# Mean and variance of the first layer norm on ACT for three of four chunks, with the order of all items changed

## The chip, the cores and the metric

One core of a Trainium2 chip runs the whole program. Time is device microseconds of one execution; what counts is the median over several runs. The engines are TensorE (PE), VectorE (DVE), ScalarE (ACT), GpSimd (POOL) and SyncE (SP, which here only issues DMAs). Each runs its own instruction list in order, and they meet through semaphores.

## What is computed

Four sequences (chunks) of 512 tokens, 128 features. Each goes through an attention-like block and a mixture of experts:

```python
mod = (_silu(c) @ wmod).reshape(4, 6, 1, -1)      # sa, ca, ga, sb, cb, gb per chunk
h = _layernorm(x) * (1 + ca) + sa
x = x + ga * attn(h)                              # rmsnorm, in-projection, two convolutions,
                                                  # gate, low-rank mixing, out-projection
h = _layernorm(x) * (1 + cb) + sb
logits = h @ router_w.T + expert_bias             # top 8 of 160, sigmoid weights, normalised
routed = sum over experts of combine * silu(h @ w_gate[e]) @ w_down[e]
x = x + gb * (routed + shared)
```

The first `_layernorm` is (x - mean) / sqrt(var + 1e-5) over the 128 features of each token.

## The kernel before, in words

A chunk is four tiles of 128 tokens (NT = 4), tokens on the partitions. The experts are taken in pairs, two pairs to a **duo**: 40 duos a chunk, 160 in all. For duo J the PE runs the up projection of two pairs (`up`, three fp16 matmuls of 128x512 each, since every fp32 operand is split into a high and a low half), ACT evicts each with silu (L859, into `s_all`), DVE multiplies by the combine weights (`gm`, L1169), ACT writes the high half (`gh`, L878, into `g_all`), DVE the low half (`gl`, L1158), and PE adds the down projection into one bank. The down projection of duo J - 4 is interleaved with the up projection of duo J (LAG = 4), gh and gl of duo J - 2 with silu and gm of duo J (HOLD = 2). There are two up banks, so an up projection waits for the silu of the duo before in its bank.

Everything else is a named **item**: `setup(n)` prepares weights, `att(c, name)` is a step of the block of chunk c or of the router, `split_hi(k)` on ACT and `split_lo(k)` on DVE turn weight piece k into its halves (20 pieces, L723 and L986). One function, `walk`, gives the order for all engines. It first lists items by hand (the start), then runs the duos, and after duo d of chunk c it takes the items in the table `WITH[c][d]`. Every engine walks this same list and emits only its own part of an item, so moving an item moves it on each engine that takes part in it. The order is fixed when the program is built.

Items that matter here, in the order of the data:

- `stat` (L987 to L1003 on DVE, L651 on POOL): for the first norm of chunk c, four BN_STATS, four BN_AGGR and `ve` = variance + 1e-5 on DVE, then POOL raises it to -0.5 (`rstd`). `nb` (L1012): -mean * rstd.
- `t1a`, `t1b` (ACT, L732), `hm`, `ha` (DVE, L1030, L1033): the normalised and modulated `h`. Chunk 0 does it on DVE alone (L1018, L1025). For chunks 1 to 3 `hm` needs the modulation rows, which `setup(20)` and `setup(22)` send through DRAM (SP: `rows_mod`, then the broadcast into `mod`, L535 and L538).
- `square` (ACT, L739, with an accumulator), `rms` (DVE L1008, POOL L654), `hi` (ACT, L744), `turn` (PE), `hnT` (ACT, L758), `low` (DVE, L1050): the rms norm and the transposed input in two halves.
- `conv`, `val`, `z`, `gate` (PE); `mid0/1` (ACT, L777) and `tap0/1:0` to `:8` (DVE, L1058 and L1065): the 9-tap convolution of each half of the features, on PE for one half of chunks 0 and 1 and on DVE for the others. `zh` (ACT), `zl` (DVE, L1082), `zmv` (SP, four DMAs, L566).
- `silu0/1` (L768, L765), `tanh0/1` (L784), `gy0/1` (DVE, L1088), `ya`, `yb`, `o0`, `o1` (PE), `x2` (DVE, L1093): the end of the block. `wo` and `base0/1` prepare it.
- `bn` (DVE, L1097), `rstd2` (POOL, L657), `nb2` (L1109), `t2a/t2b` (ACT, L793), `turn2` (PE, L1373), `xh` (ACT, L815 and L816), `xl` (DVE, L1117): the second norm, transposed, in two halves: the input of all 40 duos of the chunk.
- `logit` and `shup` (PE), `prob` (ACT, sigmoid, L822, with a table load), `max`, `sum`, `swap` (DVE), `norm` (ACT, L846), `cw` (DVE, L1142): the combine weights. For chunk 0 `c0` and `c1` (ACT L838, PE L1417) spread the weights of the first two duos. `ss`, `ssh` (ACT, L829, L832) and `ssl` (DVE) are the shared expert's input.

The start does the whole block of chunk 0 and much of that of chunk 1; the rest of chunk 1 and the blocks of chunks 2 and 3 are spread over the duos by the table.

Of the kernel before, what the change touches and what calls it, by code (L numbers as in the profile page):

```python
# [18 lines left out]
NT = L // P  # L19
# [47 lines left out]
for _n, _w in (("id", P), ("ones2", P), ("isym", L), ("esym", EDGE)):  # L67
# [11 lines left out]
        4: ((11, "split_lo"), (12, "split_hi"),),
        6: ((12, "split_lo"),),  # L80
        7: ((1, "silu1"),),
        8: ((2, "t1a"), (2, "hm"), (13, "split_lo"), (1, "yb0"), (1, "tanh0"), (3, "nb"), (1, "ya1"), (2, "t1b"),
            (13, "split_hi"),),
        10: ((2, "ha"),),
        11: ((14, "split_lo"), (14, "split_hi"), (15, "split_hi"), (15, "split_lo"), (1, "tanh1"), (1, "yb1"),),
        12: ((1, "gy0"),),
        13: ((16, "split_hi"), (1, "gy1"),),
        14: ((2, "rms"),),
# [10 lines left out]
        31: ((2, "val1"), (2, "tap0:3"), (1, "sum"),),
        33: ((1, "ss"),),  # L100
        34: ((1, "norm"),),
        35: ((1, "c_out"), (2, "tap0:4"), (1, "cw"),),
        36: ((19, "split_lo"), (2, "mid1"), (19, "split_hi"),),
        37: ((1, "cT_sb"), (1, "cT"),),
        38: ((2, "z"), (1, "ssh"), (2, "tap0:5"), (2, "zh"),),
    },
    {
        0: ((1, "ssl"), (2, "zl"),),
        3: ((2, "tap0:6"), (2, "base0"), (2, "gate"),),
        4: ((2, "tap0:7"), (2, "tanh0"), (2, "zmv"), (2, "tap0:8"), (2, "tanh1"),),  # L110
        9: ((2, "silu0"),),
        10: ((2, "tap1:0"), (3, "hm"), (2, "tap1:1"), (3, "t1b"), (3, "t1a"), (2, "ya0"),),
        11: ((3, "ha"),),
        13: ((2, "tap1:2"),),
        15: ((2, "tap1:3"),),
        16: ((3, "square"),),
        17: ((2, "tap1:4"),),
        18: ((2, "tap1:5"),),
        19: ((3, "rms"), (2, "tap1:6"),),
        20: ((2, "tap1:7"),),  # L120
        21: ((3, "hi"), (2, "tap1:8"),),
        22: ((3, "turn"),),
        23: ((2, "sxl"), (2, "silu1"), (2, "sxh"),),
        24: ((2, "gy0"), (2, "ya1"),),
        25: ((2, "wo"), (2, "yb0"), (3, "hnT"), (2, "yb1"), (2, "gy1"), (3, "low"), (2, "base1"),),
        26: ((2, "x2"),),
        27: ((2, "o0"), (2, "o1"), (2, "bn"),),
        28: ((3, "val0"), (3, "mid0"), (3, "tap0:0"), (2, "nb2"),),
        30: ((2, "t2a"),),
        31: ((2, "t2b"),),  # L130
        32: ((3, "tap0:1"), (2, "xh"), (2, "turn2"), (2, "xl"),),
        34: ((2, "prob"), (2, "logit"), (2, "max"), (2, "swap"), (3, "tap0:2"), (2, "sum"),),
        35: ((3, "val1"), (2, "shup"), (3, "tap0:3"),),
        36: ((2, "c_out"), (2, "norm"), (2, "cw"), (3, "tap0:4"),),
        38: ((2, "cT"), (2, "cT_sb"), (3, "tap0:5"), (3, "mid1"),),
        39: ((2, "ss"), (3, "tap0:6"),),
    },
    {
        0: ((2, "ssh"),),
        1: ((2, "ssl"), (3, "z"),),  # L140
        2: ((3, "zh"),),
        3: ((3, "tap0:7"),),
        4: ((3, "tap0:8"),),
        5: ((3, "tap1:0"),),
        6: ((3, "tap1:1"),),
        7: ((3, "silu0"),),
        8: ((3, "zl"), (3, "tap1:2"),),
        10: ((3, "zmv"), (3, "tap1:3"), (3, "gate"),),
        13: ((3, "tap1:4"),),
        14: ((3, "tap1:5"),),  # L150
        16: ((3, "tap1:6"), (3, "tap1:7"), (3, "ya0"),),
        18: ((3, "tap1:8"),),
        20: ((3, "wo"), (3, "silu1"), (3, "sxh"), (3, "sxl"),),
        21: ((3, "ya1"),),
        22: ((3, "base0"), (3, "yb0"), (3, "gy0"), (3, "tanh0"), (3, "yb1"), (3, "base1"), (3, "gy1"),),
        23: ((3, "tanh1"),),
        24: ((3, "x2"), (3, "o0"), (3, "o1"),),
        25: ((3, "bn"),),
        26: ((3, "nb2"),),
        28: ((3, "t2a"),),  # L160
        29: ((3, "t2b"),),
        30: ((3, "turn2"), (3, "xl"), (3, "xh"),),
        33: ((0, "table"), (3, "max"), (3, "logit"), (3, "prob"), (3, "swap"),),
        34: ((3, "sum"), (3, "shup"), (3, "ss"), (2, "rstd2"),),
        36: ((3, "norm"), (3, "cw"), (3, "c_out"),),
        38: ((3, "cT_sb"), (3, "cT"), (3, "ssl"), (3, "ssh"),),
    },
    {
        7: ((3, "rstd2"),),
# [9 lines left out]
def walk(setup, att, split_hi, split_lo, duo, end):  # L179
# [16 lines left out]
    setup(14)
    att(0, "turn")
    setup(5)
    att(1, "stat")
    setup(20)  # L200
    setup(12)
    setup(18)
    att(0, "val1")
    att(0, "low")
    att(0, "base0")
    att(0, "zmv")
# [7 lines left out]
    att(0, "hnT")
    att(0, "tap1:2")
    setup(6)
    att(0, "mid1")
    setup(13)
# [32 lines left out]
    split_lo(2)
    setup(8)
    att(0, "conv0:8:9")
    att(1, "square")
    att(1, "rms")
    att(0, "gy0")
    att(0, "gy1")
    split_lo(3)
    split_lo(4)
    att(0, "gate")  # L260
    att(1, "wo")
    att(0, "x2")
    att(1, "low")
    att(0, "bn")
    att(0, "ya0")
    split_lo(5)
    att(0, "tanh1")
# [19 lines left out]
    att(1, "val1")
    att(0, "xl")
    att(1, "hnT")
    att(1, "tap1:4")  # L290
    split_lo(8)
    split_hi(5)
    split_hi(6)
    att(1, "mid1")
    att(0, "wbh")
    split_lo(9)
    att(1, "zh")
    att(0, "max")
    att(2, "nb")
    split_hi(7)  # L300
# [4 lines left out]
    att(0, "sum")
    att(0, "swap")
    att(0, "xh")
    att(1, "conv0:0:2")
    att(1, "tap1:5")
    att(1, "conv0:2:3")  # L310
    split_hi(8)
    att(0, "turn2")
    att(0, "cw")
    att(1, "conv0:3:4")
    split_hi(9)
    att(3, "stat")
    att(1, "conv0:4:5")
# [27 lines left out]
def build(nc, x, vecs, mats, wmod_d, outT_d, consts, rows, frow_d, symT, rsgT, idf_c, w_d, out):  # L345
# [3 lines left out]
    with ExitStack() as ctx:  # L349
        def sb(name, shape, dt=F32):  # L350
            return ctx.enter_context(nc.sbuf_tensor(name, shape, dt))
# [28 lines left out]
        wo = sb("wo", [P, ML, D])  # L380
# [517 lines left out]
        def _(dve):  # L898
            e = nc.vector
# [639 lines left out]
```

## Time and profile before

| | |
|---|---|
| median of 3 runs | 521.14 us (521.12 to 522.51) |
| profiled execution, own time | 520.07 us |
| its span (first to last instruction) | 517.9 us |
| busy PE / DVE / ACT / POOL | 501.1 / 495.1 / 428.5 / 31.1 us |
| granted TensorE clock over the span | 0.995 |
| shares of the chain that ended last | PE 87%, DVE 4%, ACT 4%, DMA 2% |

The time of an execution is about 2 us more than the span of its profile. Busy time counts an engine once where two of its instructions overlap. A wait in the profile is idle time of an engine just ahead of an instruction, with what ended it. The chain of waits is followed back from the last instruction. L numbers are lines of the kernel before.

### The profile page before, as it was taken

The numbers are of one execution on the slowest core, as the hardware profiler recorded it, in microseconds if no ns is written. First come the engines' busy times: TensorE is split into PE (matmuls) and PEld (weight loads), VectorE is DVE, ScalarE is ACT, GpSimd is POOL, SyncE is SP. The second block draws the span as 40 slices with busy tenths as digits, with TensorE's granted clock in tenths as the row PEclk, the third lists the DMA queues.
The fourth block names the chain that finished last, engine by engine and source line by source line (L and its number), as shares of the span: only waits on it lengthen the run. The fifth ranks groups of instructions, "written<-read, shape, count | busy, mean of one in ns | idle before, by whom it ended". The sixth has DMA issues, their size and how long they took to land.

```text
span 517.9 us, 7227 instructions
## 1 busy us (share of the span) xinstructions
PE 501.1 (97%) x2424; PEld 241.9 (47%) x2424; DVE 495.1 (96%) x635; ACT 428.5 (83%) x701; POOL 31.1 (6%) x56
## 2 busy tenths in 40 slices
PE   7977799999999999999999999999999999999996
PEld 5643444454444444444545444445454444444442
DVE  6999999999999999999999999999999989999995
ACT  5769989988999888887699977786899877777773
POOL 7511000011000000000100000000100000000000
PEclk9999999999999999999999999999999999999999
DMA  8688375455655657555454665654663776666650
GB/s 268 250 317 345 105 224 181 174 190 178 203 161 150 243 158 259 190 195 182 146 204 123 228 205 192 207 199 140 191 204 117 266 223 203 207 200 204 200 169 20
DMA packets 33165, 101.30 MB, mean 196 GB/s; under 512 B 3684, under 2 KB 8936, under 8 KB 33128
## 3 DMA queue, kind: packets, MB, share of 16 engines
q1 hardware_dynamic: 33128, 100.84, 59.6%
q8 instruction: 19, 0.31, 0.3%
q14 instruction: 18, 0.15, 0.1%
HBM read 97.94 MB, written 2.36 MB: 194 GB/s over the span
## 4 chain that ended last, share of the span: by engine, by line
PE 87%; DVE 4%; ACT 4%; DMA 2%; issue 1%; SPq 1%; ACTq 0%; DVEq 0%
PE bank L1198 28%; PE bank L1200 27%; PE bank L1199 27%; DMA idf<-idf_dram 1%; DVE w L986 1%; PE bank L1363 1%; DMA mod<-rows_mod 1%; PE bank L1353 1%; ACT s_all L859 1%; PE bank L1209 1%; ACT w L723 1%; SPq L566 0%; DVE attw L1065 0%; ACT g_all L878 0%; PE bank L1373 0%
## 5 line engine op out<-in xcount | busy, mean ns | idle before, releaser
L859 ACT ACTIVATE s_all<-bank 128x512 f32<-128x512 f32 x320 | 188.9, 594 | 61.0 <-PE bank L1200 60.2
L1158 DVE TENSOR_TENSOR g_all<-s_all,g_all 128x1024 f16<-128x1024 f32 x160 | 194.7, 1217 | 11.0 <-ACT g_all L878 10.8
L1169 DVE TENSOR_TENSOR s_all<-s_all,c_all 128x1024 f32<-128x1024 f32 x158 | 192.2, 1216 | 0.1
L878 ACT ACTIVATE g_all<-s_all 128x1024 f16<-128x1024 f32 x160 | 168.5, 1053 | 2.8 <-DVE s_all L1169 2.4
L1198 PE MATMUL bank<-g_all,w 128*128 128x512 f16 x320 | 121.3, 379 | 0.7 <-DVE g_all L1158 0.7
L1198 PE MATMUL bank<-x_h,w 128*128 128x512 f16 x320 | 121.3, 379 | 0.4 <-ACT s_all L859 0.3
L1199 PE MATMUL bank<-g_all,w 128*128 128x512 f16 x320 | 121.3, 379 | 0.0
L1200 PE MATMUL bank<-g_all,w 128*128 128x512 f16 x320 | 121.3, 379 | 0.0
L1200 PE MATMUL bank<-x_l,w 128*128 128x512 f16 x320 | 121.3, 379 | 0.0
L1199 PE MATMUL bank<-x_h,w 128*128 128x512 f16 x320 | 121.3, 379 | 0.0
L1198 PEld LDWEIGHTS bank<-g_all,w 128*128 128x128 f16 x320 | 31.3, 98 | 40.5 <-DVE g_all L1158 4.2
L1198 PEld LDWEIGHTS bank<-x_h,w 128*128 128x128 f16 x320 | 31.3, 98 | 39.1 <-ACT s_all L859 4.3
L1200 PEld LDWEIGHTS bank<-g_all,w 128*128 128x128 f16 x320 | 31.3, 98 | 37.7
L1200 PEld LDWEIGHTS bank<-x_l,w 128*128 128x128 f16 x320 | 31.3, 98 | 37.7
L1199 PEld LDWEIGHTS bank<-g_all,w 128*128 128x128 f16 x320 | 31.3, 98 | 36.6
L1199 PEld LDWEIGHTS bank<-x_h,w 128*128 128x128 f16 x320 | 31.3, 98 | 34.5 <-issue 0.3
L1065 DVE SCALAR_TENSOR_TENSOR attw<-bank,vec,attw 128x511 f32<-128x511 f32 (+3 forms) x48 | 35.5, 740 | 0.2
L986 DVE SCALAR_TENSOR_TENSOR w<-w 128x1024 f16<-128x1024 f32 x20 | 24.1, 1216 | 0.0
L723 ACT ACTIVATE w<-w 128x1024 f16<-128x1024 f32 x20 | 20.6, 1053 | 0.0
L657 POOL TENSOR_TENSOR rstd<-ve,mhalf 128x4 f32<-128x4 f32 x4 | 7.7, 1913 | 156.0 <-DVE ve L1106 156.0
L654 POOL TENSOR_TENSOR rms<-mse,mhalf 128x4 f32<-128x4 f32 x4 | 5.3, 1334 | 156.8 <-DVE mse L1008 156.8
L1363 PE MATMUL bank<-wo,attw 128*128 128x128 f32 x64 | 7.9, 276 | 2.3 <-DVE attw L1088 2.3
(245 smaller groups left out, 383.7 us busy)
## 6 DMA issues: line engine op xcount, KB each, us to landing
c_all<-combine SPq DMA_DIRECT2D x158, 512.0 KB, 3.9
w<-w_dram SPq DMA_DIRECT2D x20, 512.0 KB, 9.5
combine<-cT SPq DMA_DIRECT2D x4, 256.0 KB, 2.0
out_dram<-res SPq DMA_DIRECT2D x3, 256.0 KB, 2.4
s_all<-mats_dram SPq DMA_DIRECT2D x1, 640.0 KB, 6.7
attw<-symT_dram SPq DMA_DIRECT2D x1, 576.0 KB, 7.7
mod<-rows_mod SPq DMA_DIRECT2D x1, 576.0 KB
res<-x_dram SPq DMA_DIRECT2D x2, 256.0 KB, 5.4
```

The costliest lines, as they stand in the source:

```text
L657: g.tensor_tensor(rstd2[:], ve2[:], mhalf[:, 0:NT], ALU.pow).then_inc(s["rstd2_set"], 1)
L723: a(high(i), staged(i), ACT.Copy, scale=ES).then_inc(s["w_hi"], 1)
L859: a(sr[J % SRING][:, q * L:(q + 1) * L], U[q][:], ACT.Silu, scale=1.0 / ES).then_inc(s["s_done"], 1)
L878: a(gh[n % GRING], sr[n % SRING], ACT.Copy).then_inc(s["hi_set"], 1)
L986: e.scalar_tensor_tensor(out=low(i), in0=staged(i), scalar=ES, in1=high(i), op0=ALU.mult, op1=ALU.subtract).then_inc(s["w_lo"], 1)
L1065: e.scalar_tensor_tensor(out=acc[:, t0:t9], in0=val[:, t0 + d:t9 + d], scalar=v("sym_k", mid + d), in1=acc[:, t0:t9], op0=ALU.mult, op1=AL ...
L1158: e.tensor_tensor(gl[n % GRING], sr[n % SRING], gh[n % GRING], ALU.subtract).then_inc(s["lo_set"], 1)
L1169: e.tensor_tensor(sr[J % SRING], sr[J % SRING], cr[J % CRING], ALU.mult).then_inc(s["gm"], 1)
L1198: mm(dst, lh, rh, start=start, stop=False)
L1199: mm(dst, ll, rh, start=False, stop=False)
L1200: return mm(dst, lh, rl, start=False, stop=stop)
L1363: last = mm(A3[:, w], gate[:, i, w], wo[:, i, :], start=(i == 0), stop=(i == ML - 1))
```

## The change

In `stat`, chunk 0 stays as it was. For chunks 1 to 3 ACT computes both moments in two passes over the four tiles, each pass with the accumulator output: the first gives mean * -1/sqrt(D) (`nm`), the second squares x/sqrt(D) + nm and sums it to the variance (`va`). ACT waits for its own first pass (`sn_set`). DVE keeps only the addition of 1e-5, and `nb` reads `nm` with a factor sqrt(D).

```diff
-        st, mv = sb("st", [P, B * NT, 6]), sb("mv", [P, B * NT, 2])
+        st, mv = sb("st", [P, NT, 6]), sb("mv", [P, NT, 2])
+        nm, va = sb("nm", [P, B * NT]), sb("va", [P, B * NT])
+        sqs = sb("sqs", [P, NT, D])
...
+            def moments(sq, xt, mean, var, first, second):
+
+                if second[1] > 2:
+                    act.wait_ge(second[0], second[1] - 1)
+                for t in range(NT):
+                    last = a(sq[:, t, :], xt[:, t, :], ACT.Identity, scale=-D ** -1.5, accum_out=mean[:, t:t + 1])
+                last.then_inc(first[0], 1)
+                act.wait_ge(*first)
+                for t in range(NT):
+                    last = a(sq[:, t, :], xt[:, t, :], ACT.Square, scale=D ** -0.5, bias=mean[:, t:t + 1],
+                             accum_out=var[:, t:t + 1])
+                last.then_inc(second[0], 1)
+
             def att(c, n):
-                if n in ("t1a", "t1b"):
+                if n == "stat" and c:
+                    w = slice(c * NT, (c + 1) * NT)
+                    act.wait_ge(s[f"x_in{min(c, 2)}"], 16)
+                    moments(sqs, res[:, w], nm[:, w], va[:, w], (s["sn_set"], c), (s["stats"], c + 1))
+                elif n in ("t1a", "t1b"):
...
                 if n == "stat":
                     w = slice(c * NT, (c + 1) * NT)
-                    dve.wait_ge(s[f"x_in{min(c, 2)}"], 16)
+                    if c:
+                        dve.wait_ge(s["stats"], c + 1)
+                        e.tensor_scalar(ve[:, w], va[:, w], 1e-5, None, ALU.add).then_inc(s["ve_set"], 1)
+                        return
+                    dve.wait_ge(s["x_in0"], 16)
...
-                    e.scalar_tensor_tensor(out=nb[:, w], in0=mv[:, w, 0], scalar=-1.0, in1=rstd[:, w], op0=ALU.mult,
+                    e.scalar_tensor_tensor(out=nb[:, w], in0=nm[:, w], scalar=D ** 0.5, in1=rstd[:, w], op0=ALU.mult,
```

The hand-written start and the whole table `WITH` are written in another order. Two lines of the table, the entries of duos 19 and 20 of chunk 0:

```diff
-        20: ((1, "rstd2"), (17, "split_lo"), (1, "bn"),),
+        19: ((1, "x2"), (1, "o0"), (1, "o1"), (17, "split_lo"), (3, "stat"),),
+        20: ((1, "bn"), (2, "turn"),),
```

Before, all three of these stats stood in the start; now chunk 3's is in duo 19 of chunk 0. The total of matmuls is the same. What moves is shown at three places. Line numbers behind the change are those of the new file.

**ACT in the start, from the transposed input of chunk 0 (hnT) to its zh (zp).** Before:

```order
L758 ACTIVATE hnT<-bank 128x512
L701 ACTIVATE edge<-bank 128x20
L777 ACTIVATE attw<-bank,edge,vec 128x504
L704 ACTIVATE c_all<-bank 128x384
L705 ACTIVATE c_all<-bank,vec 128x1
L723 ACTIVATE w<-w 128x1024
L752 ACTIVATE zp<-bank,zb 128x512
```

With the change (`sqs,nm` and `sqs,va` are the two passes of chunk 1's stat):

```order
L704 ACTIVATE edge<-bank 128x20
L778 ACTIVATE hnT<-bank 128x512
L733 ACTIVATE sqs,nm<-res 128x128 x4
L737 ACTIVATE sqs,va<-res,nm 128x128 x4
L797 ACTIVATE attw<-bank,edge,vec 128x504
L707 ACTIVATE c_all<-bank 128x384
L708 ACTIVATE c_all<-bank,vec 128x1
L772 ACTIVATE zp<-bank,zb 128x512
```

The stat of chunk 1 now stands ahead of mid1 (`attw<-bank,edge,vec`), and the first weight split (`w<-w`) has gone behind zh.

**ACT around the square of chunk 1 (hr,ms), up to its hnT and on to t2 of chunk 0, and with the change to zh of chunk 1 behind it.** Before:

```order
L739 ACTIVATE hr,ms<-h 128x128 x4
L784 ACTIVATE attw<-bank,inb 128x512
L723 ACTIVATE w<-w 128x1024 x2
L744 ACTIVATE hr<-h,rms 128x128 x4
L758 ACTIVATE hnT<-bank 128x512
L723 ACTIVATE w<-w 128x1024 x2
L777 ACTIVATE attw<-bank,edge,vec 128x504
L797 ACTIVATE wb_h<-wb 128x512
L752 ACTIVATE zp<-bank,zb 128x512
L723 ACTIVATE w<-w 128x1024
L793 ACTIVATE h<-res,nb,rstd 128x128 x4
```

With the change:

```order
L759 ACTIVATE hr,ms<-h 128x128 x4
L733 ACTIVATE sqs,nm<-res 128x128 x4
L737 ACTIVATE sqs,va<-res,nm 128x128 x4
L726 ACTIVATE w<-w 128x1024
L764 ACTIVATE hr<-h,rms 128x128 x4
L778 ACTIVATE hnT<-bank 128x512
L726 ACTIVATE w<-w 128x1024 x2
L813 ACTIVATE h<-res,nb,rstd 128x128 x4
L797 ACTIVATE attw<-bank,edge,vec 128x504
L772 ACTIVATE zp<-bank,zb 128x512
```

Chunk 2's stat stands between square and hi (`hr<-h,rms`), and mid1 and zh of chunk 1 have gone from ahead of t2 (`h<-res,nb,rstd`) to behind it. On DVE the same stretch, around gy of chunk 0 (`attw<-attw,bank`) and up to the second norm's ve (before) or low of chunk 1 (`hnT<-bank,hnT`, with the change), was:

```order
L1008 TENSOR_SCALAR mse<-ms 128x4
L1088 SCALAR_TENSOR_TENSOR attw<-attw,bank 128x512 x2
L986 SCALAR_TENSOR_TENSOR w<-w 128x1024 x2
L1072 SCALAR_TENSOR_TENSOR wo<-outT,mod 128x256
L1077 TENSOR_TENSOR gob<-brow,mod 128x128
L1093 TENSOR_TENSOR res<-bank,res 128x512
L1050 TENSOR_TENSOR hnT<-bank,hnT 128x512
L1097 BN_STATS st<-res 128x6 x4
L1101 BN_AGGR mv<-st 128x2 x4
L1106 TENSOR_SCALAR ve<-mv 128x4
```

and is now:

```order
L1112 SCALAR_TENSOR_TENSOR attw<-attw,bank 128x512
L1006 SCALAR_TENSOR_TENSOR w<-w 128x1024
L1112 SCALAR_TENSOR_TENSOR attw<-attw,bank 128x512
L1032 TENSOR_SCALAR mse<-ms 128x4
L1006 SCALAR_TENSOR_TENSOR w<-w 128x1024
L1147 TENSOR_TENSOR wb_l<-wb,wb_h 128x512
L1117 TENSOR_TENSOR res<-bank,res 128x512
L1121 BN_STATS st<-res 128x6 x4
L1125 BN_AGGR mv<-st 128x2 x4
L1130 TENSOR_SCALAR ve<-mv 128x4
L1006 SCALAR_TENSOR_TENSOR w<-w 128x1024
L1074 TENSOR_TENSOR hnT<-bank,hnT 128x512
```

The end of chunk 0 (gy, x2 as `res<-bank,res`, bn) has gone ahead of wo, gob and low of chunk 1, and wb_l stands there now.

**ACT from c0 (the first spread, h<-cw) to the first high half (g_all) of the duos.** Before:

```order
L838 ACTIVATE h<-cw 128x512
L838 ACTIVATE t<-cw 128x512
L852 ACTIVATE cT<-bank 128x512
L854 ACTIVATE cT<-bank 32x512
L838 ACTIVATE x<-cw 128x512
L838 ACTIVATE yT<-cw 128x512
L723 ACTIVATE w<-w 128x1024
L768 ACTIVATE attw<-bank 128x512
L859 ACTIVATE s_all<-bank 128x512 x2
L832 ACTIVATE ssx<-ss 128x512
L859 ACTIVATE s_all<-bank 128x512
L878 ACTIVATE g_all<-s_all 128x1024
```

With the change:

```order
L858 ACTIVATE h<-cw 128x512
L858 ACTIVATE t<-cw 128x512
L872 ACTIVATE cT<-bank 128x512
L874 ACTIVATE cT<-bank 32x512
L726 ACTIVATE w<-w 128x1024
L879 ACTIVATE s_all<-bank 128x512 x2
L858 ACTIVATE x<-cw 128x512
L858 ACTIVATE yT<-cw 128x512
L726 ACTIVATE w<-w 128x1024
L788 ACTIVATE attw<-bank 128x512
L879 ACTIVATE s_all<-bank 128x512
L898 ACTIVATE g_all<-s_all 128x1024
```

One more weight split stands in this stretch, the silus of duo 1 (`s_all<-bank`, x2) come ahead of c1 (`x<-cw`, `yT<-cw`), and ssh (`ssx<-ss`) has gone ahead of it.

## Rows read from the trace of the kernel before

**Rows 1.** The page of the kernel before: span, busy time of each engine.

```profile
span 517.9 us, 7227 instructions
...
PE 501.1 (97%) x2424; PEld 241.9 (47%) x2424; DVE 495.1 (96%) x635; ACT 428.5 (83%) x701; POOL 31.1 (6%) x56
```

**Rows 2.** Busy us of PE, PEld, DVE, ACT, POOL by stretch; clock, DMA share, GB/s.

```profile
14.80:60.00 45.20, 36.31 (x196) 20.67 (x195) 43.36 (x100) 36.90 (x72) 10.80 (x12) 1.00 0.67 255
60.00:505.00 445.00, 444.59 (x2133) 208.80 (x2132) 433.38 (x486) 377.00 (x595) 8.66 (x5) 1.00 0.60 192
64.00:143.00 79.00, 78.91 (x369) 37.13 (x370) 78.83 (x86) 72.07 (x119) 3.83 (x2) 1.00 0.59 192
```

**Rows 3.** Waits of PE, 14.8 to 64 us: total, times, longest.

```profile
PE bank L1363 <- DVE attw L1088: 2.3, 1, 2.3
PE bank L1402 <- DVE cw L1142: 1.8, 1, 1.8
PE bank L1373 <- ACT h L793: 1.7, 2, 1.4
PE bank L1198 <- DVE hnT L1050: 1.6, 1, 1.6
```

**Rows 4.** Waits of PE, 64 to 505 us.

```profile
PE bank L1198 <- ACT s_all L859: 0.3, 1, 0.3
```

**Rows 5.** Timeline of DVE, 376 us: start, duration, its first idle time since 64.

```profile
376.41 1.23 DVE L1158 TENSOR_TENSOR g_all<-s_all,g_all 128x1024 f16<-128x1024 f32 x1 [0.23 <-ACT g_all L878]
```

**Rows 6.** Timeline of DVE, 13 to 55 us.

```profile
13.13 0.87 DVE L996 BATCH_NORM_STATS2 st<-res 128x6 f32<-128x128 f32 x4
...
14.53 1.35 DVE L936 TENSOR_TENSOR wc_l<-attw,wc_h 128x1152 f16<-128x1152 f32 x1
...
31.06 0.69 DVE L1030 TENSOR_TENSOR h<-h,mod 128x512 f32<-128x512 f32 x1 [0.98 <-DMA mod<-rows_mod]
...
44.42 1.22 DVE L986 SCALAR_TENSOR_TENSOR w<-w 128x1024 f16<-128x1024 f32 x1
45.55 0.74 DVE L1065 SCALAR_TENSOR_TENSOR attw<-bank,vec,attw 128x511 f32<-128x511 f32 x1
...
51.28 1.00 DVE L1133 MAX8 mx<-pr 128x8 f32<-128x160 f32 x4
...
54.69 0.83 DVE L1142 SCALAR_TENSOR_TENSOR cw<-key,cw 128x640 f32<-128x640 f32 x1
```

**Rows 7.** ACT by line and shape, 0 to 64 us: busy, mean ns of one.

```profile
L744 ACT ACTIVATE hr<-h,rms 128x128 f32<-128x128 f32 x8 | 2.5, 388 | 0.0
L739 ACT ACTIVATE hr<-h 128x128 f32<-128x128 f32 x8 | 2.4, 297 | 2.0 <-DVE h L1033 1.4 <-DVE h L1025 0.6
```

**Rows 8.** Timeline of ACT, 33 to 47 us.

```profile
33.02 0.29 ACT L739 ACTIVATE hr<-h 128x128 f32<-128x128 f32 x1
...
33.32 0.29 ACT L739 ACTIVATE hr<-h 128x128 f32<-128x128 f32 x1
...
38.58 0.60 ACT L758 ACTIVATE hnT<-bank 128x512 f16<-128x512 f32 x1 [0.95 <-PE bank L1288]
...
43.88 1.65 ACT L793 ACTIVATE h<-res,nb,rstd 128x128 f32<-128x128 f32 x4
...
46.74 0.77 ACT L816 ACTIVATE x_h<-bank,sbc,cbc 128x512 f16<-128x512 f32 x1
```

**Rows 9.** Timeline of SP's DMA issues, 23 to 27 us.

```profile
23.79 2.68 SPq L566 DMA_DIRECT2D zs<-zp  x4
26.51 0.58 SPq L538 DMA_DIRECT2D mod<-rows_mod  x1
```

**Rows 10.** The chain of waits that ended last, at 64 and 104 us.

```profile
63.55 0.49 ACT s_all L859
64.09 0.39 PE bank L1198
...
104.47 1.78 PE bank L1363 x16
```

More of the change, by code:

```diff
@@ L79 @@
[L79 to L88, printed above, removed]
@@ L99 @@
[L99 to L105, printed above, removed]
-    },
-    {
[L108 to L129, printed above, removed]
-        31: ((2, "t2b"),),
[L131 to L136, printed above, removed]
-    },
@@ L138 @@
-    {
[L139 to L158, printed above, removed]
-        26: ((3, "nb2"),),
[L160 to L166, printed above, removed]
@@ L183, in walk @@
     setup(2)
-    setup(30)
-    setup(31)
     setup(1)
-    setup(16)
+    setup(20)
     att(0, "hm")
     att(0, "ha")
-    setup(15)
+    att(0, "zmv")
+    setup(22)
+    setup(16)
+    setup(10)
+    att(0, "square")
     att(0, "rms")
-    setup(10)
-    setup(17)
-    att(0, "square")
     setup(9)
     setup(14)
-    att(0, "turn")
[L198 to L206, printed above, removed]
@@ L207, in walk @@
-    att(0, "wo")
-    att(0, "base1")
+    setup(5)
+    setup(30)
+    setup(18)
+    setup(31)
+    setup(4)
+    setup(15)
+    att(0, "low")
+    setup(17)
+    att(0, "base0")
+    att(0, "wo")
+    setup(23)
+    att(0, "hi")
+    setup(6)
+    att(0, "base1")
+    att(0, "turn")
+    att(0, "hnT")
     att(0, "tap1:0")
     att(0, "tap1:1")
-    setup(4)
-    att(0, "hi")
-    att(1, "nb")
[L214 to L218, printed above, removed]
+    att(1, "stat")
@@ L251, in walk @@
[L251 to L267, printed above, removed]
+    att(1, "hm")
+    att(1, "t1b")
+    att(1, "ha")
+    att(0, "gy0")
+    att(0, "c_out")
+    split_lo(2)
+    att(0, "z")
+    att(0, "gy1")
+    att(0, "silu0")
+    att(0, "conv0:2:4")
@@ new lines, in walk @@
+    att(0, "silu1")
+    att(0, "conv0:4:5")
+    setup(3)
+    att(1, "rms")
+    att(0, "tanh0")
+    att(0, "tanh1")
+    att(0, "rstd2")
+    split_hi(2)
+    split_lo(3)
+    att(0, "conv0:5:7")
+    att(0, "wbl")
+    att(0, "conv0:7:8")
+    att(0, "x2")
+    att(0, "conv0:8:9")
+    att(0, "gate")
+    att(0, "bn")
+    split_lo(4)
+    split_hi(3)
+    att(1, "low")
+    att(1, "wo")
+    att(0, "nb2")
+    att(0, "ya0")
+    att(0, "yb0")
+    split_lo(5)
+    att(1, "square")
+    att(2, "stat")
@@ L286, in walk @@
+    att(1, "z")
     att(1, "tap1:3")
[L287 to L292, printed above, removed]
-    split_hi(6)
[L294 to L300, printed above, removed]
+    split_hi(6)
     att(0, "t2a")
     att(0, "t2b")
-    att(1, "z")
-    att(1, "zmv")
[L305 to L310, printed above, removed]
@@ L311, in walk @@
-    split_hi(8)
[L312 to L317, printed above, removed]
+    att(0, "turn2")
+    split_lo(7)
+    split_lo(8)
+    att(0, "max")
+    att(1, "conv0:0:2")
+    att(1, "tap1:4")
+    att(1, "mid1")
+    att(0, "sum")
+    att(1, "conv0:2:3")
+    att(1, "zh")
+    att(1, "conv0:3:4")
+    att(0, "logit")
+    att(0, "swap")
+    att(1, "tap1:5")
+    att(0, "xh")
+    att(1, "conv0:4:5")
+    split_hi(7)
+    att(0, "shup")
```

182 lines of the change are left out of this document (124 added, 58 removed).

## The prediction

> **What bounds the kernel now.** I read the page's engine line first. TensorE (PE) is busy 97% of 517.9 us, DVE 96%, ACT 83% [rows 1]. A mean over stages does not say which engine sets the end, so I cut the span into stretches. From 60 to 505 us PE is busy 444.59 of 445 us [rows 2], and its only wait there is 0.3 us [rows 4]. So the expert stretch is full of TensorE work, and its length is that work. The change adds and removes no matmul. Both orders hold the same ones, and only their places differ. Before the takeover, from 14.8 to 60 us, PE is busy 36.31 of 45.2 us [rows 2]. The four largest waits there are 7.4 us: 2.3 for gy (L1088), 1.8 for cw (L1142), 1.7 for t2 (L793), 1.6 for low (L1050) [rows 3]. Time can be won only there, or in the drain behind 505 us, which the change leaves alone. In the same stretch DVE is busy 43.36 of 45.2 us and ACT 36.90 [rows 2]. So DVE paces the start and ACT has 8.3 us of slack. DVE then has no idle time until 376.41 us [rows 5]. In the expert stretch it only just keeps up with PE.
>
> I mark the takeover by one event: the up projection of duo 3 (second half) starts at 64.09, released by the ACT silu of duo 2 at 63.55 [rows 10]. From there to 505 us PE waits at most 0.3 us, and both kernels have the same matmuls left. So the time saved is how much earlier this event comes, less whatever stalls appear later.
>
> **The change part by part.** Durations of neighbours on one engine overlap a little, so I cost an item by the step from its start to the next start.
>
> *Off DVE.* Chunk 1's stat is four BN_STATS, four BN_AGGR and ve. It holds DVE from 13.13 to 14.53 [rows 6], 1.40 us. Three of them go, 4.2 us. What stays is an addition of 128x4 each, about 0.08 us by the last item inside those 1.40 us. Net 4.0 us, all of it ahead of the first gl.
>
> *Onto ACT.* Each stat becomes four Identity and four Square, all with an accumulator read. The existing square of chunk 1 is the nearest row: starts at 33.02 and 33.32 [rows 8], so 0.30 us a piece, or 1.2 for the first pass. The second pass has a pointer for its bias. An ACTIVATE with one pointer takes 388 ns, one with immediates 297 [rows 7], so the step is 0.39 and the pass 1.55. Between the passes ACT waits for its own last read; I put 0.15 there. That is 2.9 us for a stat. The lower end is no cost for the pointer, 2.4. The upper end takes the steps of t2, with two pointers (1.65 us for four, [rows 8]), plus a read each: 3.3. I take 2.9, since one pointer is what the code has. The start gets two of these, 5.8 us, and chunk 3's falls into duo 19 of chunk 0. Up to the first gh and gl both engines split the same number of weight pieces as before.
>
> *First checkpoint, the mod broadcast.* Chunk 1's stat stands on ACT between hnT and mid1 of chunk 0. The second DVE tap chain needs mid1. It could be late by 0.8 us, but DVE has base and wo in front of it, so it starts 0.25 to 0.3 us later. Between its start and zl a weight split (1.13 us, from 44.42 to 45.55) gives way to a tap (0.66) and an addition (0.08) [rows 6], so 0.4 us are saved. Zl, and with it the zmv on SP, comes about 0.1 us earlier. The mod broadcast is queued behind zmv on SP (23.79 and 26.51, [rows 9]) and DVE's hm of chunk 1 waits for its landing (31.06, idle 0.98, [rows 6]). POOL is free of chunk 1's power sooner and has the gate rows ready a microsecond earlier, but zmv still blocks SP. **So 2.8 us of the saving on DVE have no use here: hm starts at about 30.95.** DVE fills the time with other work and waits for the DMA.
>
> *Second checkpoint, DVE from hm to max.* Before, 31.06 to 51.28 is 20.2 us without a gap [rows 6]. Setup 8 (0.9), one tap (0.66) and one split (1.13) leave this stretch; wb_l (0.6) and ve (0.08) enter. 20.2 - 2.0 = 18.2, so DVE alone would reach max at 49.1, 2.1 us earlier.
>
> *The same stretch on ACT.* Square of chunk 1 now starts at 32.45 and takes 1.2. Chunk 2's stat (2.9) and one split (0.95) stand between it and hi (1.2). HnT of chunk 1 comes at 39.1 instead of 38.58 [rows 8], 0.5 later. DVE has x2 and bn of chunk 0 moved ahead of low, so that does not hurt. The saving comes from there. bn ends some 2.5 us sooner, POOL's rstd2 and nb2 follow at about 41.0, and ACT, after two splits, starts t2 at 41.5 instead of 43.88 [rows 8], 2.4 us earlier. Behind t2 now stand mid1 and zh (1.3 us) that stood ahead before, so x_h starts at 45.05 instead of 46.74, 1.7 earlier. Two splits, the table load, prob, the second load, ss, ssh (0.5, moved ahead) and norm follow. Norm starts at about 51.95 and ends at 53.2. DVE gets max at 49.7, swap by 52.9, and a tap put ahead of cw. Cw starts at 53.7 instead of 54.69 [rows 6], **1.0 us earlier**.
>
> *Third checkpoint, cw to the takeover.* On ACT from c0 to the first gh one split enters (0.95) and ssh (0.5) is gone. 1.0 - 0.4 = **0.6 us**: the takeover comes at about 63.5.
>
> *After it.* DVE reaches its first gl about 2 us sooner, PE 0.6 sooner, so DVE's lead grows by 1.4. By duo 18 DVE has one split (1.13) and base0 of chunk 2 (0.6) more. It is about where it was, with no new stall. ACT by duo 18 has one split and the third stat more, 3.85 us. Over 64 to 143 us it has 79 - 72.07 = 6.9 us of idle time [rows 2]. The stat in duo 19 is next to o0 and o1, which give PE 1.78 us of its own work [rows 10]. I cost it at nothing; without that cover it would cost up to 2 us.
>
> The sum is -0.6 us. The profiled execution took 520.07 us, 2.1 more than its span, and becomes 519.5. The median of the runs, 521.14, is 1.1 above it and becomes **520.5 us**. With 2.4 for a stat both checkpoints on ACT's way move by 0.4 to 0.5, giving -1.3; with 3.3 about 0.
>
> A rule speaks against the change. The Trainium skill (ScalarE: Activation LUTs, section Rules for kernel authors) says that additions and multiplications belong on VectorE, not ScalarE. The trace agrees on the price, 1.40 against 2.9. By it alone each stat would lose 1.5 us where the engines are equally short of time, 4.5 us in all; that is the direction of the second rival.
>
> **The rivals.** *Faster, 518.7 us.* ACT absorbs the stats in its 8.3 us of idle time and DVE's own 2.1 to 2.5 us at max carry through to the takeover, 521.14 - 2.4. For it: DVE was the full engine. Against it: with 5.8 us more, ACT has about 2.5 us of slack left, and the load of prob's table cannot start before x_h and two splits. Some of it (over 1.6 us, my bound) would do.
>
> *Slower, 523.5 us.* ACT becomes the bound in the expert stretch. Each up projection needs the silu of the duo before in its bank. Up to the 28th gh ACT gets 3.85 us more and also two table loads and prob, 3.4 us, that now stand ahead of that gh: 7.2 us against 6.9 of idle time [rows 2]. Where these items stand closer than PE's own extra work covers, PE waits, and a lost microsecond never returns since PE is full. The saving is lost and 3 us added if two blocks of 2.5 to 3 us are half covered. It decides once stalls pass 2.2 us. For it: DVE's lead has no reserve either [rows 5]. Against it: the table loads only move by a duo, and stat 3 has o0 and o1.
>
> *No change, 521.1 us.* The stats cost 3.3 or low of chunk 1, late by half a microsecond, stalls the chain to zl and x_l. The engine set free waits for the engine loaded.
>
> **How the numbers follow.** A measurement of this kernel can tell about 0.3%, 1.6 us, from no change; my forecast lies inside that. Forecast (0.3 to 1.5 us faster) 0.42, no change 0.12, the faster rival 0.30, the slower one 0.16. Within 0.3% are the first two, 0.54. The range goes from 518.5 (the faster rival's value, a little past) to 522.3 (a slower case half-way), leaving out somewhat under 2 in 10.
>
> **What would show it.** The steps are right if, in the new profile, the accumulating groups on ACT take 1.2 and 1.55 us a pass; if DVE's hm of chunk 1 still waits for the mod broadcast near 31 us, with more idle time; if t2 starts near 41.5, x_h near 45, cw near 53.7, and the takeover's silu ends near 63.4; and if PE from 64 to 505 us still waits under 0.5 us in total. I am wrong if hm starts before 30 (then SP's order is not the limit), if cw comes before 52.5, or if PE shows waits for s_all (L859's successor) or g_all in the expert stretch, above all near duos 4 to 9 and 19 to 30 of chunk 0.

## Result and profile after

The changed kernel takes **524.58 us** (median of 8 runs, 522.74 to 525.82), the kernel before, on the same chip, 521.78 (8 runs, 520.27 to 523.13). The ratio is 1.0061, with a 95% interval of 1.0045 to 1.0077. It is slower by 2.8 us, where I forecast 0.6 us faster and gave 0.16 to slower. A second measurement of the same code (a1, below) gave 1.0052 (1.0034 to 1.0070). One execution each of two later kernels, b1 (762 us) and b3 (1371 us, the profiled one), ran far slower than all others and is left out of their times and readings.

The page, beside [rows 1]:

```profile
span 523.7 us, 7253 instructions
...
PE 506.4 (97%) x2424; PEld 245.0 (47%) x2424; DVE 492.6 (94%) x611; ACT 435.7 (83%) x749; POOL 39.8 (8%) x56
```

DVE fell by 2.5 us and ACT rose by 7.2: the directions that I had costed, each by some 1.5 us less than my 4.0 and 8.7. POOL, whose instructions the change does not touch, rose by 8.7. That is the first sign. The stretches of the changed kernel, in the columns of [rows 2], with one more cut:

```profile
14.80:60.00 45.20, 39.25 (x196) 21.96 (x195) 42.59 (x90) 41.89 (x105) 13.63 (x14) 0.95 0.68 254
60.00:505.00 445.00, 440.62 (x2109) 207.28 (x2110) 428.92 (x481) 375.34 (x606) 16.70 (x6) 1.00 0.58 190
95.00:115.00 20.00, 17.12 (x69) 7.30 (x68) 17.09 (x17) 15.47 (x26) 9.86 (x1) 0.91 0.49 159
```

And the last of them in the kernel before:

```profile
95.00:115.00 20.00, 20.00 (x102) 10.04 (x101) 20.00 (x21) 18.21 (x36) 1.91 (x1) 1.00 0.52 180
```

From 60 to 505 us PE is no longer full. Of the 4.4 us that it is idle, 2.9 lie in these 20 us; most of the rest is the wait for x (L858), which comes before the takeover and only falls behind the 60 us cut here. In the 20 us one single POOL instruction is busy for 9.86 us. The waits of the changed kernel from 60 to 510 us say how the two are tied:

```profile
ACT hr L764 <- POOL rms L657: 4.2, 1, 4.2
PE bank L1222 <- ACT s_all L879: 3.1, 2, 2.9
```

The timeline of POOL, and of DVE from the instruction that releases it:

```profile
96.64 9.86 POOL L657 TENSOR_TENSOR rms<-mse,mhalf 128x4 f32<-128x4 f32 x1 [50.38 <-DVE mse L1032]
```

```profile
96.40 0.16 DVE L1032 TENSOR_SCALAR mse<-ms 128x4 f32<-128x4 f32 x1
96.47 1.22 DVE L1182 TENSOR_TENSOR g_all<-s_all,g_all 128x1024 f16<-128x1024 f32 x1
97.60 1.22 DVE L1193 TENSOR_TENSOR s_all<-s_all,c_all 128x1024 f32<-128x1024 f32 x1
98.74 1.22 DVE L1006 SCALAR_TENSOR_TENSOR w<-w 128x1024 f16<-128x1024 f32 x1
...
104.42 1.22 DVE L1006 SCALAR_TENSOR_TENSOR w<-w 128x1024 f16<-128x1024 f32 x1
105.55 0.68 DVE L1112 SCALAR_TENSOR_TENSOR attw<-attw,bank 128x512 f32<-128x512 f32 x1
106.15 1.22 DVE L1006 SCALAR_TENSOR_TENSOR w<-w 128x1024 f16<-128x1024 f32 x1
```

This is the power of the rms norm of chunk 2 (`rms`; the expectations below call it the second norm). It is 128x4 elements, and where DVE lets it through it takes 1.01 us, as at 223.84 us of this trace. Here it starts 0.17 us into a run of eight DVE instructions, each of 1.14 us and each with two operands in SBUF, without a gap. It ends 0.27 us after gy1 (L1112) does, the first instruction behind it whose second operand is in PSUM. In the kernel before, the same power stood elsewhere in the order:

```profile
103.59 1.91 POOL L654 TENSOR_TENSOR rms<-mse,mhalf 128x4 f32<-128x4 f32 x1 [45.59 <-DVE mse L1008]
```

What hangs on it is read on ACT and on PE of the changed kernel:

```profile
106.53 1.28 ACT L764 ACTIVATE hr<-h,rms 128x128 f32<-128x128 f32 x4 [4.24 <-POOL rms L657]
107.72 0.57 ACT L879 ACTIVATE s_all<-bank 128x512 f32<-128x512 f32 x1
```

```profile
105.09 0.38 PE L1224 MATMUL bank<-g_all,w 128*128 128x512 f16 x1
108.35 0.61 PE L1222 MATMUL bank<-x_h,w 128*128 128x512 f16 x1 [2.88 <-ACT s_all L879]
108.75 0.63 PE L1223 MATMUL bank<-x_h,w 128*128 128x512 f16 x1
```

ACT takes its work in order. hi of chunk 2 (L764) waits 4.24 us for the power, the silu (L879) stands behind hi, and the next up projection waits 2.88 us for the silu. Behind the wait PE's matmuls start some 0.42 us apart instead of 0.22 and take 0.61 instead of 0.38: the granted clock is at its lower level (1.2 GHz) until about 111.6 us. The chain of waits, which in [rows 10] had only PE here, now runs through POOL:

```profile
96.40 0.17 DVE mse L1032
96.57 0.07 issue
96.64 9.87 POOL rms L657
...
106.84 0.97 ACT hr L764 x3
107.81 0.49 ACT s_all L879
```

**The start.** The rows that answer to [rows 6] and [rows 8] are, on DVE:

```profile
7.98 0.35 DVE L943 TENSOR_SCALAR s_all<-s_all,vec 128x256 f32<-128x256 f32 x1 [2.38 <-DMA s_all<-mats_dram]
...
32.61 0.69 DVE L1054 TENSOR_TENSOR h<-h,mod 128x512 f32<-128x512 f32 x1 [1.13 <-DMA mod<-rows_mod]
...
55.31 0.82 DVE L1166 SCALAR_TENSOR_TENSOR cw<-key,cw 128x640 f32<-128x640 f32 x1
```

and on ACT, by line and shape:

```profile
L737 ACT ACTIVATE sqs<-res,nm 128x128 f32<-128x128 f32 x12 | 4.7, 390 | 0.1
L733 ACT ACTIVATE sqs<-res 128x128 f32<-128x128 f32 x12 | 3.5, 299 | 0.0
```

The takeover comes at 65.11 us, 1.02 later than before. The DMA that brings mats_dram landed late in this execution (DVE idle 2.38 us; in the profile of before 0.67). From hm of chunk 1 to the takeover it is 32.50 us; before it was 33.03. The span is 5.8 us longer: 1.0 up to the takeover and 4.7 behind it.

The late landing is chance, since a1 shows 0.68 us of idle time there with the same code, but it is not the whole of the late takeover. Nine profiles share this start (this one, a1 to a3, b1, b2 and c1 to c3; b3 is left out). Their takeovers fall into two groups: 62.74 to 63.65 us in six of them, 64.72 to 65.11 in this one, a2 and c2. In a2 and c2 the landing was early (DVE idle 0.60 and 0.78 us), and in b1 and c3, of the early group, it was late (1.51 and 1.52). What the three late ones share is TensorE's granted clock in the first 20 us. PE's busy time, then clock, DMA share and GB/s, from 8 to 20 us in this profile, a2, c2 and a1:

```profile
8.00:20.00 12.00, 10.43 (x57) 0.72 1.03 362
8.00:20.00 12.00, 11.13 (x61) 0.72 1.02 361
8.00:20.00 12.00, 10.81 (x58) 0.72 1.01 358
8.00:20.00 12.00, 10.12 (x66) 1.00 1.02 362
```

The other five have 0.86 or 1.00. So the start alone moves by up to 2.4 us from one execution to the next, whatever the change does. That the lower clock is the cause of the later takeover is not shown: no run isolates it.

### The profile page after: what moved, and what is told of

Read it like the earlier page. It is cut to its first block, busy times and chain, and to the rows that moved or that the text cites. A ratio compares the mean times of both kernels' runs of the same rounds, so it can differ in the third digit from the quotient of the medians.

```text
span 523.7 us, 7253 instructions
## 1 busy us (share of the span) xinstructions
PE 506.4 (97%) x2424; PEld 245.0 (47%) x2424; DVE 492.6 (94%) x611; ACT 435.7 (83%) x749; POOL 39.8 (8%) x56
## 4 chain that ended last, share of the span: by engine, by line
PE 78%; POOL 2%; DVE 2%; issue 1%; ACT 1%; ACTq 0%; DVEq 0%
PE bank L1222 25%; PE bank L1224 25%; PE bank L1223 25%; POOL rms L657 2%; PE bank L1387 1%; DVE g_all L1182 1%; DVE s_all L1193 0%; PE bank L1500 0%; PE bank L1426 0%; PE bank L1429 0%; PE bank L1397 0%; ACT g_all L898 0%; ACT hr L764 0%; PE bank L1312 0%; PE bank L1411 0%
## 5 line engine op out<-in xcount | busy, mean ns | idle before, releaser
L879 ACT ACTIVATE s_all<-bank 128x512 f32<-128x512 f32 x320 | 188.6, 594 | 61.4 <-PE bank L1224 60.9
L657 POOL TENSOR_TENSOR rms<-mse,mhalf 128x4 f32<-128x4 f32 x4 | 14.9, 3713 | 162.8 <-DVE mse L1032 162.8
```

The costliest lines, as they stand in the source:

```text
L657: g.tensor_tensor(rms[:], mse[:], mhalf[:, 0:NT], ALU.pow).then_inc(s["rms_set"], 1)
L879: a(sr[J % SRING][:, q * L:(q + 1) * L], U[q][:], ACT.Silu, scale=1.0 / ES).then_inc(s["s_done"], 1)
```

## Experiments

Three theories went in. **A**: VectorE's run of two-input instructions keeps POOL's power from SBUF; the power holds ACT, ACT holds PE. **B**: ACT's added work bounds the expert stretch (my rival). **C**: the later landing, and the rest too, is chance. Two more came with the later runs. **D**: any short instruction or shift in time would have let the power in. **E**: it is decided anew at each hand-over from one two-input instruction to the next. All ratios are to the kernel before, measured beside.

### a1_same: the changed kernel again

No edit.

> The changed kernel once more, nothing edited. Theory A (GpSimd's power of the second norm of chunk 2 is kept off SBUF by VectorE's unbroken run of instructions with two SBUF inputs, holds ScalarE's hi, and that holds the up projection): the power of chunk 2 takes 8 to 10 us again, the up projection near 108 us waits about 3 us, and the time is 2.5 to 4.5 us over before. Rival B (ScalarE's extra work of the statistics bounds the expert stretch): the time is over before by the same, whatever the power takes. Rival C (the 1.5 us later landing of the weights of the first reduction was chance, and the rest too): the power takes 2 us, no wait near 108 us, and the time is within 1 us of before.

Measured: 523.87 us, 1.0052 (1.0034 to 1.0070). The power took 9.86 us again, ACT waited 4.2 us for it and PE 2.88. DVE on the start:

```profile
30.24 0.69 DVE L1054 TENSOR_TENSOR h<-h,mod 128x512 f32<-128x512 f32 x1 [0.81 <-DMA mod<-rows_mod]
...
52.93 0.83 DVE L1166 SCALAR_TENSOR_TENSOR cw<-key,cw 128x640 f32<-128x640 f32 x1
```

This time mats_dram landed as in the profile of before, and the takeover came at 62.74, 1.35 us ahead of it. So C holds for the start and falls for the power. This span, 520.4, is the cleaner one for the sum: -1.35 up to the takeover, +3.85 behind it, +2.5 in all. PE's clock stayed at 1.00 in 95 to 115 us here, where it was 0.91 in the first profile; the stretch from the takeover to PE's last wait is 0.9 us shorter (450.66 against 451.55).

### a2_break: four one-input instructions behind the mean square

```diff
  e.tensor_scalar(mse[:], ms[:], 1e-6, None, ALU.add).then_inc(s["mse_set"], 1)
+ if c == 2:
+     for t in range(NT):
+         e.bn_stats(spare[:, t, :], outT[:, t % 2, :])
```

> The changed kernel with four statistics of one SBUF input (about 0.23 us each, on a tile that nobody reads) on VectorE right behind the mean square of chunk 2, so that its run of two-input instructions is broken for about 0.9 us just when GpSimd's power starts. Theory A: the power takes 2 us or less, ScalarE does not wait for it, no wait of the up projection near 108 us, and the time is 4 to 5 us below the changed kernel, so 0 to 1.5 us below before. Rival B: ScalarE's load is unchanged and VectorE has 0.9 us more, so the time stays or rises by up to 1 us. Rival C: the same as the changed kernel within 1 us.

Measured: 521.07 us, 0.9995 (0.9980 to 1.0009). POOL, then DVE:

```profile
96.35 1.01 POOL L658 TENSOR_TENSOR rms<-mse,mhalf 128x4 f32<-128x4 f32 x1 [50.51 <-DVE mse L1033]
```

```profile
96.18 0.86 DVE L1036 BATCH_NORM_STATS2 spare<-outT 128x6 f32<-128x128 f32 x4
```

**More work on the fullest helper made the kernel 2.8 us faster** than a1, on the same chip. The power took 1.01 us and neither ACT nor PE waited for it; PE's longest wait near 108 us was 0.4. The size is below the 4 to 5 us that I expected: between 95 and 115 us PE is busy 19.55 us instead of 17.12. B and C fall.

At a second place this trace shows the same lock-out. The power of chunk 3's `rstd` (L655) began at 118.83 us, 0.17 into a two-input instruction, and took 3.05 us: past a second one, until the statistics of one input at 120.93. No instruction waited for it, so it cost nothing.

### a3_late: hi of chunk 2 two duos later

```diff
- 15: ((16, "split_hi"), (1, "yb1"), (2, "hi"), (15, "split_lo"), ...
+ 15: ((16, "split_hi"), (1, "yb1"), (15, "split_lo"), ...
- 17: ((18, "split_hi"),),
+ 17: ((18, "split_hi"), (2, "hi"),),
```

> The changed kernel with ScalarE's hi of chunk 2 (the four scalings that need the power) moved from duo 15 to duo 17 of chunk 0, everything else as it is. Theory A, and that the harm comes only through ScalarE's in-order wait: the power still takes 8 to 10 us, but ScalarE no longer waits for it (under 0.5 us), the up projection runs on without its 3 us wait, and the time falls by 3 to 5 us. If the power's length alone did not matter but VectorE were slowed too, it would fall by less than 2 us. Rival B: no change over 0.5 us, since ScalarE does the same work.

Measured: 520.56 us, 0.9988 (0.9976 to 0.9999). The power is as long as ever, but nothing hangs on it, and what is left of PE's wait is 0.7:

```profile
94.71 9.86 POOL L657 TENSOR_TENSOR rms<-mse,mhalf 128x4 f32<-128x4 f32 x1 [50.40 <-DVE mse L1032]
```

```profile
PE bank L1222 <- ACT s_all L879: 0.7, 1, 0.7
```

So the harm came through ACT's in-order wait alone. Against the changed kernel that is 3.3 us (523.87 to 520.56, on one chip). With ACT's statistics and this order, the kernel is 0.1% faster than before, at the edge of what these runs resolve.

### a4_old_order: the statistics on ACT, the order of before

The tables WITH and the walk of the kernel before, the rest from the changed kernel.

> The statistics by ScalarE, in the order of items of the kernel before. Theory A: the power of chunk 2 meets the neighbours that it had before and takes about 2 us; the time is then before's plus what ScalarE's 2.9 us do where they stand: in the start, where the items of chunk 1 and 2 were placed for VectorE, up to 1 us more or less; so 520 to 524. Rival B: ScalarE's three statistics cost their whole 2.9 us each on the path where PE is full, so 3 to 9 us over before.

Measured: 529.23 us, 1.0147 (1.0125 to 1.0169). The power took 1.92 us, and PE had no wait over 0.3 us behind the takeover. The loss is in the start: the takeover came at 73.97, 9.9 later than before, and the stretch behind it is 0.6 longer. DVE from 14 to 70 us waits for ACT's passes, and for prob behind them:

```profile
DVE ve L1015 <- ACT sqs L736: 4.7, 2, 3.0
DVE mx L1156 <- ACT pr L841: 2.9, 1, 2.9
```

The chain of waits of this kernel, in the same stretch:

```profile
13.96 0.59 ACT sqs L732 x4
14.57 1.65 ACT sqs L736 x8
...
55.98 1.18 ACT sqs L732 x8
57.18 1.65 ACT sqs L736 x8
```

I had expected up to 1 us either way, or 3 to 9 with B. The size is B's, but the place is the start and not the expert stretch. In this execution mats_dram also landed late (2.23 us) and PE's granted clock was 0.50 from 14 to 20 us, so not all of the 9.9 us need be ACT's passes; the loss in the medians is 7.7. The statistics on ACT need the new order.

### b1_two_inputs: the control for a2

```diff
+ if c == 2:
+     for t in range(NT):
+         e.tensor_tensor(sqs[:, t, :], outT[:, 0, :], outT[:, 1, :], ALU.mult)
```

> Control for the four spare statistics: the same place behind the mean square of chunk 2, again four short VectorE instructions (128x128), but products with two SBUF inputs, written to a tile that nobody reads at that time. Theory A (only an instruction with one SBUF input lets GpSimd in once it has been passed over): the power of chunk 2 again lasts 9 to 11 us, until gy1 runs, ScalarE waits 4 to 5 us for it, and the time is that of the changed kernel or up to 1 us over it (523.5 to 526). Rival D (any short instruction, or any shift of the phase, would have let the power through): the power takes 2 us or less and the time is near 521, as with the statistics.

Measured: 525.87 us, 1.0088 (1.0068 to 1.0108).

```profile
95.00 0.89 DVE L1035 TENSOR_TENSOR sqs<-outT 128x128 f32<-128x128 f32 x4
```

```profile
95.17 10.67 POOL L657 TENSOR_TENSOR rms<-mse,mhalf 128x4 f32<-128x4 f32 x1 [50.38 <-DVE mse L1032]
```

Four instructions as short as those of a2, in the same place, with two SBUF operands instead of one: the power is 0.81 us longer instead of 8.85 shorter. ACT waited 5.0 us. What lets POOL in is the kind of instruction, not its length or a shift in time. D falls.

### b2, c1, c2, c3: the power at other places of the run

Mean square and power of chunk 2 move from duo 12 to 11, 13, 14, and in c3 right ahead of gy1 in duo 15, there with hi in duo 17.

```diff
- 12: ((15, "split_hi"), (2, "rms"),),
+ 11: ((2, "rms"),),                       (b2)
+ 13: ((14, "split_lo"), (2, "rms"),),     (c1)
+ 14: ((2, "rms"), (1, "tanh1"),),         (c2)
+ 15: (..., (15, "split_lo"), (2, "rms"), (1, "gy1"), ...   (c3)
```

> The changed kernel with mean square and power of chunk 2 one duo earlier (duo 11). VectorE's run without a one-input instruction stays as long, so if GpSimd is always passed over in such a run (A), the power lasts 11 to 13 us and still ends with gy1, and the time is that of the changed kernel. If being passed over is a matter of how the hand-over falls (rival E), the power may end after one instruction, at about 1.9 us as in seven other places of these traces, and the time is near 521.

> The power of chunk 2 in duo 13 once more, for its profile. A (once GpSimd is passed over it gets in only at the next VectorE instruction with one SBUF input): from the five instructions of 1.14 us that then still stand ahead of gy1, 0.17 us after the first began, 5.7 - 0.17 + 0.86, about 6.4 us, ending 0.27 us after gy1. E (the hand-over decides anew each time): 1.9 us.

> The power of chunk 2 in duo 14, three instructions of the run ahead of gy1. A: 3.4 - 0.17 + 0.86, about 4.1 us, ending 0.27 us after gy1, since what lets it in has not moved. E: 1.9 us, as it was at duo 14 of the kernel before.

> The changed kernel with mean square and power of chunk 2 right ahead of gy1 in duo 15 (no work added) and hi of chunk 2 in duo 17. A: the power runs beside gy1 and takes 1.0 us, ScalarE does not wait, no wait of the up projection over 0.7 us near 108 us; 3 to 4 us below the changed kernel, so 0.3 to 1.2 us below before (520 to 521). If the wait at 108 us had another cause it would stay, and the time be 523 or more.

POOL's timeline of the four, in this order:

```profile
92.18 12.13 POOL L658 TENSOR_TENSOR rms<-mse,mhalf 128x4 f32<-128x4 f32 x1 [48.11 <-DVE mse L1033]
```

```profile
98.21 6.46 POOL L657 TENSOR_TENSOR rms<-mse,mhalf 128x4 f32<-128x4 f32 x1 [53.81 <-DVE mse L1032]
```

```profile
101.92 4.18 POOL L657 TENSOR_TENSOR rms<-mse,mhalf 128x4 f32<-128x4 f32 x1 [56.04 <-DVE mse L1032]
```

```profile
104.09 1.01 POOL L657 TENSOR_TENSOR rms<-mse,mhalf 128x4 f32<-128x4 f32 x1 [59.47 <-DVE mse L1032]
```

With ten, eight, five, three and no two-input instructions between it and gy1 the power takes 12.13, 9.86, 6.46, 4.18 and 1.01 us. Each instruction more costs 1.14 us, which is its step on DVE, and in the four long cases the power ends 0.26 to 0.27 us behind gy1. In c3 it starts beside gy1 (103.91 to 104.61 us) and waits for nothing. E falls for this stretch: there is no hand-over between two two-input instructions in it. The times are 523.77 us for b2 (1.0057; 1.0035 to 1.0080), one run each for c1 and c2 (523.13 and 525.55), all with ACT waiting 4.2 us and PE 2.9 as in the changed kernel, since gy1, which ends the power, did not move. An earlier kernel with the edit of c1, b3, had been timed:

> The changed kernel with mean square and power of chunk 2 one duo later (duo 13), five instructions of the run still ahead of gy1. A: the power lasts 5 to 7 us and ends with gy1; ScalarE's wait and the time are those of the changed kernel. E: 1.9 us, the wait gone or under 1 us, and the time near 521.

It took 524.53 us, 1.0074 (1.0051 to 1.0097), which is A's for the time. It has no profile that can be read beside the others, so the length of its power was taken from c1.

c3 adds no work and took 520.62 us, 0.9990 (0.9975 to 1.0006): the same as a3 within its interval, 3.2 us below the changed kernel as a1 measured it. PE's wait near 108 us is 0.6.

### b4 and c4: the order without the arithmetic

b4 is the changed kernel with the statistics of chunks 1 to 3 on DVE again; c4 is b4 with the edit of a3.

```diff
- if n == "stat" and c:
-     ...
-     moments(sqs, res[:, w], nm[:, w], va[:, w], (s["sn_set"], c), (s["stats"], c + 1))
...
- st, mv = sb("st", [P, NT, 6]), sb("mv", [P, NT, 2])
+ st, mv = sb("st", [P, B * NT, 6]), sb("mv", [P, B * NT, 2])
```

> The order of items of the changed kernel, but all statistics by VectorE as before, so that the difference to the changed kernel is the arithmetic alone. Theory A: the order makes the stall, so the power of chunk 2 is again long (8 to 10 us) and the time 523 to 526, within 1.5 us of the changed kernel. Rival B (ScalarE's passes cost it): 2 to 4 us below the changed kernel, and no wait near 108 us.

> Statistics by VectorE, the changed kernel's order, hi of chunk 2 in duo 17: the order without the arithmetic and without the stall. From the same kernel with the stall (5.6 us over before) less the 3 to 4 us that moving hi gave: 1.5 to 2.5 us over before, all of it before 65 us, as against 0.5 us below before with ScalarE's statistics. If the order alone were as good as before's, it would be within 0.8 us of before.

Measured: b4 526.68 us, 1.0118 (1.0097 to 1.0139), its power 9.86 us and PE's wait 2.9; c4 524.97 us, 1.0061 (1.0035 to 1.0086), with a takeover at 67.35. Neither the stall nor its size has to do with who computes the statistics: B falls again. c4 came out above the 1.5 to 2.5 us that I expected; in its profile the takeover is 3.3 us late and the stretch behind it 1.6 us longer (448.44 against 446.81), where I had expected all of the loss ahead of 65 us. With a3 and a4 the four corners stand together, in us against the kernel before, from the ratios and its 521 us:

| | order of before | new order, stalled | new order, hi in duo 17 |
|---|---|---|---|
| statistics by DVE | 0 | +6.1 (b4) | +3.2 (c4) |
| statistics by ACT | +7.7 (a4) | +2.7 to +3.2 | -0.6 (a3) |

Either half alone loses 3 to 8 us. Together, with the stall away, they are worth -0.6 (-1.3 to -0.1).

## Why the prediction was wrong

**Right: the prices of a statistic.** 299 and 390 ns by line, steps of 0.30 and 0.39, and 2.85 us from 17.27 to 20.12 for chunk 1's, where I had 2.9 from [rows 7, 8].

**Right: from hm of chunk 1 to the takeover.** I had 30.95 to 63.5, 32.55 us; both profiles of the changed kernel show 32.50, and the seven others with this start 32.49 to 32.62. Hm does wait for the mod broadcast (1.13 and 0.81 us idle), so most of DVE's saving has no use ahead of it; "with more idle time" was not borne out, as it was 0.98 before. In a1, max started at 48.98 and cw at 52.93; I had 49.7 and 53.7, both 0.7 to 0.8 later, as was hm.

**Not settled: the first checkpoint.** "Zl, and with it the zmv on SP, comes about 0.1 us earlier." In a1 hm started at 30.24, 0.8 us ahead of 31.06, not 0.1; in the first profile it was at 32.61, and the other seven lie between. With such a spread, one profile of the kernel before does not fix this term to half a microsecond. I had taken the start of one execution as the start of the kernel, and had no term for the granted clock there. That the medians of a3 and c3 lie 0.5 to 0.6 us below before, where their spans are 0.3 and 0.5 above that of its profile, fits this: the profiled execution of before was 1.1 us below its median.

**The step that failed: "It is about where it was, with no new stall."** I counted busy time of each engine and ACT's idle time against it, and costed what ACT and DVE gain and lose. Behind the takeover POOL was in no term: I put it at nothing because the change takes no work from it and gives it none. I had noted that DVE runs without idle time until 376 us [rows 5] and used it only as a lack of reserve. It is also what POOL's operand reads meet. The new order moved mean square and power of chunk 2 from duo 14 to 12 and hi from duo 16 to 15 of chunk 0, and put the power at the head of eight two-input instructions. It measured 9.86 us instead of 1.91, then 4.2 us on ACT and 2.9 on PE. Against a3, which has this order without the stall (447.93 us from the takeover to PE's last wait), the stall costs 2.7 us in a1 (450.66) and 3.6 in the first profile (451.55), where the clock fell too; by the medians of a1 and a3 it is 3.3. The sign of being wrong that I had named, PE waiting for s_all in the expert stretch, did come.

**The rivals.** Slower was the right sign, but that 523.5 lies near the measured 524.58 is luck. Its own sum, the saving lost and 3 us added to 521.1, gives 524.1 and not 523.5, and its reason was another: "Where these items stand closer than PE's own extra work covers, PE waits." ACT did hold PE, behind duo 15 and not at duos 4 to 9 or 19 to 30; but ACT was not loaded there, it waited. ACT's statistic of chunk 3 in duo 19 cost nothing that a profile shows. The rule of the Trainium skill (ScalarE: Activation LUTs, Rules for kernel authors) that I set against the change points to the slower side for a reason that the new order does not bear out: there ACT's statistics gain 3 to 4 us over DVE's. In the old order the direction is the rule's: there they lose 7.7.

The Trainium skill has the rule that does bear on it, and I did not weigh it: by its page SBUF — State Buffer, section Who interferes with whom, a VectorE instruction with two SBUF inputs and a GpSimd instruction that reads SBUF exclude each other. The runs agree: 1.01 us beside four one-input statistics, 10.67 beside four two-input products.

**What stays open.** In the traces of before and of a1 a power that started 0.17 us into a two-input DVE instruction got in at the end of that one ten times (1.91 us), six of them with the next product of the expert stretch right behind. The power of chunk 2 did so in duo 14 of the old order (before, and 1.92 in a4), and not in duo 14 of the new order (c2, 4.18), with the same three instructions behind it on DVE. Waits on semaphores, forms and gaps look alike in both. In a2 the `rstd` of chunk 3 was passed over once in the same way (3.05 us), so it is not a matter of this one stretch. No run here tells what decides it. Nor is it settled what the new order, freed of the stall, still loses behind the takeover: 1.1 us in a3 and c3 (447.9 against 446.8), of which PE's wait near 108 us is 0.6 to 0.7. And why ACT's statistics gain only in the new order, by 3 to 4 us, and lose in the old one is measured as a sum and not taken apart.

## What to carry to other kernels

When a reordering moves a small GpSimd instruction, look at what VectorE runs beside it, not at GpSimd's busy share: put it next to a VectorE instruction with one SBUF operand, or keep its reader several steps away from an in-order engine's urgent work. If an untouched engine's busy time rises in the new profile, find the one instruction whose time grew before you compare anything else. Take the start from several profiles where its clock varies. And cost both halves of a change that moves arithmetic and order together; here each alone was worse than both.

## What the runs showed of the hardware

- A power of 128x4 elements on GpSimd took 1.01 us beside one-input VectorE work and up to 12.13 us beside ten two-input instructions in a row. VectorE showed no delay: its steps stayed at 1.14 us. What let the power in was gy1, with one operand in PSUM, or statistics with one input.
- A wait of PE of 2.88 us was followed by about 3.3 us at the lower clock level (1.2 GHz) in some executions (clock of 95 to 115 us 0.91 in the first profile, b2 and c2) and not in others (1.00 in a1, c1 and b4). By the stretch from the takeover to PE's last wait the lower clock goes with 1.0 us more: 451.55, 451.67 and 451.66 us with it, 450.66 and 450.67 without (a1, c1).
- With the same code up to there, PE's granted clock from 8 to 20 us was 0.72 in three of nine executions and 0.86 or 1.00 in six. The takeover of the three came at 64.72 to 65.11 us, that of the six at 62.74 to 63.65.
